# First-layer norms as fused VectorE operations, all masks added by GpSimd, and three of four transposed probability tiles copied by ScalarE

## The chip, the core and the metric

The kernel runs on one core of one Trainium2 chip. Its time is the device time of one execution in microseconds (us); the time before is the median of three runs. A core has TensorE (the matrix engine, PE in the profile, its weight loads PEld), VectorE (DVE), ScalarE (ACT), GpSimd (POOL) and SyncE (SP), which here only issues transfers. The engines run their own instruction queues in order and wait for each other by semaphores.

## The reference

Eight sequences of 512 tokens and width 512 go through four layers. Layer 0 is an adapter with a norm, layer 1 attention and a feed-forward part, layer 2 a feed-forward part with per-sequence weights, layer 3 a stencil. The change touches the two norms ahead of attention and the softmax of attention:

```python
# layer 0
hidden = gelu(x @ down_W.T + down_b)                     # 512 x 128
hidden = hidden @ Wsel + bsel + domain_emb               # expert chosen per sequence
x = hidden @ up_W.T + up_b + x
x = (x - mean(x)) * rsqrt(var(x) + 1e-5) * ln_gamma + ln_beta         # norm 0
# layer 1
x = (x - mean(x)) / sqrt(var(x) + 1e-5) * (1 + scale) + shift         # norm 1
q, k, v = x @ Wq + bq, x @ Wk + bk, x @ Wv + bv          # 16 heads of 32
scores = q @ k.T / sqrt(32) + attention_bias             # per head 512 x 512
scores = where(src_mask, -inf, scores)
ctx = softmax(scores) @ v
x = x + ctx @ Wo + bo
...
```

## The kernel before

The program is two passes. `attention_pass` does layer 0 and attention, sequence by sequence, in a loop of eight iterations; `ffn_pass` does the rest and isn't touched. The first pass runs from about 67 us to 1101 us of the profiled span; ahead of it a prologue prepares weights and does layer 0 and both norms of the first sequence.

**An iteration.** TensorE projects q, k and v, then goes through 20 slots (`SLOTS_ALL`). Slots 0 to 15 each score one query tile of 128 rows for four heads: slot u belongs to head group u // 4 and query tile u % 4. In slot u TensorE makes four score tiles (`scores(u)`, banks 0 to 3 of PSUM), VectorE reads each, adds the bias and takes the minimum of the negated row (line 1000, output `tiles` and `nmax`), and ScalarE exponentiates (line 792). One slot later TensorE transposes the four 128x512 probability tiles (`turn`, line 651; the last of the four yet a slot later), an engine copies each transposed bank into `pT`, and TensorE multiplies by v (`values`, line 642). Beside this, slots carry work listed in `BESIDE`: the projections of the next head groups (slots 2, 3, 6, 7, 10, 11), and layer 0 of the *next* sequence (xT, down, expert, up in slots 0 to 5). VectorE takes the norm's statistics of the next sequence in slots 5 and 6 (norm 0) and 10 and 11 (norm 1). After slot 19 come the output products and the transposes of the normed next sequence.

**The bias.** SyncE loads the attention bias in halves of a slot (two heads, 128x1024 float32, 512 KB), 32 halves per iteration, into a ring of six buffers (`stage`, named `bias` in the code). Half n+6 is issued as soon as VectorE has scored half n.

**The mask.** Half of it goes by GpSimd: for the first half of each slot (heads 0 and 1) GpSimd adds the mask to the bias in place (line 508). For heads 2 and 3 TensorE first writes the mask into the bank by an identity product (line 625) and the scores accumulate on it.

**The norms of the next sequence.** After the statistics, GpSimd computes 1/sqrt(var) by ten small dependent operations and four more (`rstd_of_norm`), ScalarE scales each 128x512 tile (line 724), and GpSimd multiplies by the gain and adds the shift (lines 488 and 489). In the prologue VectorE does the same by `rstd_first` and `norm_first` (lines 917 to 926), two operations per tile.

**The copies into `pT`.** Of the four tiles of a slot VectorE copies 0 and 1 (line 1015) and ScalarE 2 and 3 (line 778).

**What sets the order.** Each engine's program is written out in slot order. Scores of slot u+1 go to the same four banks, so TensorE claims each after VectorE scored that tile of slot u. The bank ring of three for everything else is fixed by `attention_slots`.

Of the kernel before, what the change touches and what calls it, by code (L numbers as in the profile page):

```python
# [26 lines left out]
ALU = mybir.AluOpType  # L27
ACT = mybir.ActivationFunctionType
# [6 lines left out]
LINKS_A = 18  # L35
# [56 lines left out]
def pv_parts(u):  # L92
# [11 lines left out]
ACT_L0 = {8: (("scale0", 0), ("scale0", 1)), 9: (("scale0", 2), ("scale0", 3)),  # L104
          13: (("scale1", 0),), 14: (("scale1", 1),), 16: (("scale1", 2), ("scale1", 3))}
DVE_L0 = {5: (("stats0", 0), ("stats0", 1)), 6: (("stats0", 2), ("stats0", 3)),
          10: (("stats1", 0), ("stats1", 1)), 11: (("stats1", 2), ("stats1", 3))}
POOL_L0 = {2: (("up_bias",),), 9: (("rstd", 0),), 10: (("gain0", 0), ("gain0", 1)), 11: (("gain0", 2), ("gain0", 3)),
           14: (("rstd", 1),)}
# [35 lines left out]
def attention_pass(nc, a, ada_rows, x2_dram, stage, stage_in):  # L145
# [7 lines left out]
    with ExitStack() as ctx:  # L153
# [74 lines left out]
        shift = sb("shift", [P, T], F32)  # L228
# [32 lines left out]
        pool_chain = sem("pool_chain")  # L261
        pool_carrier = sem("pool_wait_carrier")
# [10 lines left out]
        rstd_ready = sem("rstd_ready")  # L273
        scaled0 = sem("scaled0")
        ln0_ready = sem("ln0_ready")
        scaled1 = sem("scaled1")
# [3 lines left out]
        pT_ready = [sem("pT_first_two_ready"), sem("pT_last_two_ready")]  # L280
# [26 lines left out]
        def read_by(key):  # L307
# [5 lines left out]
                    "T": (pT_ready[k // 2], H * T // 2, k % 2), "R": (rinv_T_ready, G, k),  # L313
                    "ctx": (ctx_ready, G, k), "wo": (x2_ready, T, k)}[name]

        def claim(pe, it, key):
# [5 lines left out]
            if last[0] == "T":  # L322
                k += last[1] * T // 2
# [124 lines left out]
        def _(pool):  # L448
# [7 lines left out]
            count = [0]  # L456

            def pool_link(base, ins):
                count[0] += 1
                ins.then_inc(pool_chain, 1)  # L460
                pool.wait_ge(pool_chain, base + count[0])

            def rstd_of_norm(base, q, which):

                def link(ins):
                    pool_link(base, ins)
                    pool.sem_inc(pool_carrier, 1)
# [15 lines left out]
            def gain(it, base, which, t):  # L483

                q = before_it(it)
                times, plus = ((ln_g[:, :], ln_b[:, :]), (ada[:, 0, :], ada[:, 1, :]))[which]
                pool.wait_ge((scaled0, scaled1)[which], q * T + t + 1)
                pool_link(base, pool.tensor_tensor(xin[:, t, :], xin[:, t, :], times, ALU.mult))
                pool.tensor_tensor(xin[:, t, :], xin[:, t, :], plus, ALU.add).then_inc((ln0_ready, x1_ready)[which], 1)

            up_bias(None)
            before_loop = count[0]
            POOL_LINKS = 2 * 15 + 2 * T
            pool.wait_ge(rows_out, 16)
            with pool.Fori(0, B) as it:
                base = before_loop + it * POOL_LINKS
                count[0] = 0

# [6 lines left out]
                for u in range(NQ):  # L505
                    n = 2 * u
# [3 lines left out]
                    for part in POOL_L0.get(u, ()):  # L510
                        if part[0] == "up_bias":
                            up_bias(it)
                        if part[0] == "rstd":
                            rstd_of_norm(base, it + 1, part[1])
# [1336 lines left out]
```

## Time and profile before

| | |
|---|---|
| median of three runs | 2616.97 us (2615.83 to 2617.12) |
| profiled execution | 2614.7 us, its span 2612.9 us |
| busy share of the span | PE 96%, DVE 76%, ACT 44%, POOL 40% |
| granted TensorE clock, mean | 0.989 of full speed |
| chain that ended last | PE 39%, DVE 9%, issue 6%, ACT 1%, POOL 1% |
| one iteration of the attention loop | 129.3 us (the mask conversion, line 958, starts at 67.0 us in the first and at 972.1 us in the last: 905.1 / 7) |

The busy share is an average over both passes. What the loop does has to be read in a stretch of the loop: which engine is never idle there, and how long each engine needs for a slot. A timeline row is: start in us, duration in us, engine, line, operation, output and inputs, count, and in brackets the idle time before it and what ended it. Two instructions of one engine may overlap by the pipeline, so the cost of one in a row of equal ones is the distance of the starts and not its duration.

### The profile page before, as it was taken

Reading aid. Unit: us, or ns where it says so; the run is one execution under the profiler, and the core shown is the slowest. Engines: PE = TensorE matmul, PEld = TensorE weight load, DVE = VectorE, ACT = ScalarE, POOL = GpSimd, SP = SyncE. Lnnn points to the kernel's source line nnn. Section 1 sums busy time; section 2 is a strip of 40 time slices with the busy share of each in tenths; the row PEclk is TensorE's granted clock in tenths of the full one; section 3 lists DMA queues with packets and bytes.
Section 4 is the critical chain, followed back from the end, with each engine's and each line's share of the span. In section 5 each row is a group of like instructions: output and inputs, shape, how many; then the busy total and the mean of one; then the engine's idle time right before and its main releaser. Section 6 shows DMA issues by size and latency. Waiting matters only on the chain.

```text
span 2612.9 us, 47096 instructions
## 1 busy us (share of the span) xinstructions
PE 2497.7 (96%) x14495; PEld 1237.5 (47%) x14583; DVE 1980.6 (76%) x3863; ACT 1147.6 (44%) x2189; POOL 1038.3 (40%) x887
## 2 busy tenths in 40 slices
PE   6999999999999999869999999999999999999996
PEld 4455555555555555434444444444444444444443
DVE  7877777777777777777878688678687786886787
ACT  3666666667666767633322223223222222232331
POOL 1464646464646464524234133143242340431430
PEclk8999999999999999989999999999999999999998
DMA  6444444454545444452322232142222222322340
GB/s 208 144 154 157 156 151 160 146 162 147 167 145 166 146 160 147 141 179 93 113 82 86 90 107 96 54 137 89 90 93 101 98 77 82 130 89 77 102 159 23
DMA packets 155507, 320.56 MB, mean 123 GB/s; under 512 B 17474, under 2 KB 23234, under 8 KB 155218
## 3 DMA queue, kind: packets, MB, share of 16 engines
q1 hardware_dynamic: 145426, 299.13, 34.6%
q10 hardware_dynamic: 9792, 17.83, 1.9%
q8 instruction: 151, 2.47, 0.4%
q14 instruction: 138, 1.13, 0.1%
HBM read 298.85 MB, written 17.86 MB: 121 GB/s over the span
## 4 chain that ended last, share of the span: by engine, by line
PE 39%; DVE 9%; issue 6%; ACT 1%; POOL 1%; DMA 1%; DVEq 0%; ACTq 0%; POOLq 0%
PE ffn_bank L1371 12%; PE ffn_bank L1373 12%; PE ffn_bank L1372 12%; PE ffn_bank L1357 2%; DVE g2T_hi L1686 1%; DVE f L1569 1%; POOL stage L1298 1%; ACT g L1512 1%; DVE stats L1554 1%; PE ffn_bank L1437 1%; PE ffn_bank L1378 1%; DVE w_lo L1656 1%; DVE stage L1597 1%; DVE f L1572 0%; DMA stage<-in_W 0%
## 5 line engine op out<-in xcount | busy, mean ns | idle before, releaser
L1000 DVE CUSTOM_DVE_ANT_0 tiles<-bank,stage 128x512 f32<-128x512 f32 x512 | 323.9, 686 | 79.4 <-PE bank L628 74.8
L792 ACT ACTIVATE tiles<-tiles,nmax 128x512 f32<-128x512 f32 x512 | 363.5, 714 | 44.5 <-DVE nmax L1000 44.4
L508 POOL TENSOR_TENSOR stage<-stage,mask_add 128x1024 f32<-128x1024 f32 x128 | 272.6, 2141 | 203.1 <-DMA stage<-in_bias 183.9
L651 PE MATMUL bank<-ident,tiles 128*128 128x128 f32 x2048 | 300.2, 280 | 16.6 <-ACT pT L778 4.4
L1686 DVE CAST g2T_hi<-g 128x512 f16<-128x512 f32 x256 | 164.8, 644 | 188.7 <-ACT g L1512 181.1
L651 PEld LDWEIGHTS bank<-ident,tiles 128*128 128x128 f32 x2048 | 222.6, 140 | 176.4 <-issue 83.2
L1298 POOL TENSOR_TENSOR stage<-grid,f 128x512 f32<-128x512 f32 x96 | 150.5, 1594 | 284.4 <-DMA grid<-in_grids 175.1
L1687 DVE TENSOR_TENSOR g2T_lo<-g,g2T_hi 128x512 f16<-128x512 f32 x256 | 245.6, 959 | 8.8
L1512 ACT ACTIVATE g<-ffn_bank,bi 128x512 f32<-128x512 f32 x128 | 88.1, 688 | 360.1 <-PE ffn_bank L1373 349.7
L1371 PE MATMUL ffn_bank<-w_hi,g2T_hi 128*128 128x512 f16 x512 | 195.3, 382 | 28.3 <-DVE g2T_lo L1687 28.0
L778 ACT ACTIVATE pT<-bank 128x512 f32<-128x512 f32 x256 | 151.1, 590 | 150.1 <-PE bank L651 150.1
L1312 POOL TENSOR_TENSOR x<-x2n,b 128x512 f32<-128x512 f32 x32 | 39.5, 1269 | 442.3 <-DVE f L1714 442.3
L1305 POOL TENSOR_TENSOR stage<-grid,f 128x512 f32<-128x512 f32 x64 | 106.4, 1681 | 267.0 <-DVE stage L1623 139.6
L1371 PE MATMUL ffn_bank<-x3T_hi,wl_hi 128*128 128x512 f16 x512 | 194.3, 379 | 5.6 <-DVE stage L1631 5.6
L1371 PE MATMUL ffn_bank<-x3T_hi,w_hi 128*128 128x512 f16 x512 | 194.3, 379 | 3.4 <-DVE x3T_lo L1653 3.3
L1372 PE MATMUL ffn_bank<-w_lo,g2T_hi 128*128 128x512 f16 x512 | 195.1, 381 | 0.0
L1373 PE MATMUL ffn_bank<-w_hi,g2T_lo 128*128 128x512 f16 x512 | 195.1, 381 | 0.0
L1372 PE MATMUL ffn_bank<-x3T_lo,w_hi 128*128 128x512 f16 x512 | 194.2, 379 | 0.0
L1371 PE MATMUL ffn_bank<-wl_hi,g2T_hi 128*128 128x512 f16 x512 | 194.0, 379 | 0.0
L1372 PE MATMUL ffn_bank<-wl_lo,g2T_hi 128*128 128x512 f16 x512 | 194.0, 379 | 0.0
L1373 PE MATMUL ffn_bank<-wl_hi,g2T_lo 128*128 128x512 f16 x512 | 194.0, 379 | 0.0
L1373 PE MATMUL ffn_bank<-x3T_hi,w_lo 128*128 128x512 f16 x512 | 194.0, 379 | 0.0
(289 smaller groups left out, 5195.1 us busy)
## 6 DMA issues: line engine op xcount, KB each, us to landing
stage<-in_bias SPq DMA_DIRECT2D x256, 512.0 KB, 4.1
stage<-in_W_l SPq DMA_DIRECT2D x128, 512.0 KB, 3.3
grid<-in_grids SPq DMA_DIRECT2D x160, 256.0 KB, 3.3
xin<-in_x SPq DMA_DIRECT2D x36, 256.0 KB, 4.1
out<-stage ACTq DMA_DIRECT2D x36, 256.0 KB, 2.0
x_rows<-tiles ACTq DMA_DIRECT2D x32, 256.0 KB, 3.0
stage<-in_W SPq DMA_DIRECT2D x16, 512.0 KB, 4.9
x2n<-x_rows SPq DMA_DIRECT2D x8, 1024.0 KB, 7.0
```

Of the source, the lines that this page charges most:

```text
L508: pool.tensor_tensor(bias[:, n % NB, :, :], bias[:, n % NB, :, :], mask_add[:, u % T, :].unsqueeze(1).to_broadcast([P, 2, S]), ALU.add).th ...
L651: mm = pe.transpose(bank[:, t * P:(t + 1) * P], tiles[:, 4 * (u % NR) + i, t * P:(t + 1) * P], ident[:, :])
L778: act.activation(pT[:, (u // 2) % 2, i, :, (u % 2) * P:(u % 2 + 1) * P], bank[:, :].rearrange("p (t q) -> p t q", t=T), ACT.Copy).then_inc ...
L792: act.activation(tile, tile, ACT.Exp, scale=-1.0, bias=nmax[:, u % 2, i:i + 1], accum_out=rsum[:, j, h:h + 1]).then_inc(prob_ready, 1)
L1000: dve.tensor_tensor_reduce(tiles[:, 4 * (u % NR) + i, :], bank[:, :], bias[:, half % NB, i % 2, :], -1.0, 3.0e38, ALU.add, ALU.min, nmax[: ...
L1298: pool.tensor_tensor(prod[:, i, :], grid[:, i, :], f[:, t, :], ALU.mult).then_inc(alpha_prod, 1)
L1371: pe.matmul(out, w[0], x[0], start=first, stop=False)
L1372: pe.matmul(out, w[0], x[1], start=False, stop=False)
L1373: return pe.matmul(out, w[1], x[0], start=False, stop=last)
L1512: act.activation(g32[:, n % 2, :], bank[:, :], func, scale=1.0 / WS, bias=vec[:, n % NF:n % NF + 1]).then_inc(gelu_ready, 1)
L1686: link(dve.tensor_copy(gT[0][:, n % 4, :], g32[:, n % 2, :]))
L1687: dve.tensor_tensor(gT[1][:, n % 4, :], g32[:, n % 2, :], gT[0][:, n % 4, :], ALU.subtract)\
```

## The change

It does five things. (1) The two norms of the next sequence leave GpSimd and ScalarE: VectorE computes 1/sqrt(var) with eleven small operations (`norm_root`) in slots 7 and 12, and does each tile with two fused operations (`norm_tile`) in slots 8 and 9 (norm 0, two tiles a slot) and 13 to 16 (norm 1, one tile a slot). (2) GpSimd adds the mask to both halves of each slot's bias. (3) TensorE's two identity products per slot go. (4) VectorE copies only transposed tile 0, ScalarE tiles 1, 2 and 3. (5) GpSimd's addition of the up-bias moves from slot 2 to behind the masks of slot 4.

```diff
-ACT_L0 = {8: (("scale0", 0), ("scale0", 1)), ...
-DVE_L0 = {5: ..., 6: ..., 10: ..., 11: ...}
-POOL_L0 = {2: (("up_bias",),), 9: (("rstd", 0),), 10: (("gain0", 0), ("gain0", 1)), 11: (("gain0", 2), ("gain0", 3)),
-           14: (("rstd", 1),)}
+DVE_L0 = {5: (("stats0", 0), ("stats0", 1)), 6: (("stats0", 2), ("stats0", 3)), 7: (("rstd", 0),),
+          8: (("norm0", 0), ("norm0", 1)), 9: (("norm0", 2), ("norm0", 3)),
+          10: (("stats1", 0), ("stats1", 1)), 11: (("stats1", 2), ("stats1", 3)), 12: (("rstd", 1), ("ada", 0)),
+          13: (("norm1", 0),), 14: (("norm1", 1),), 15: (("norm1", 2),), 16: (("norm1", 3),)}
...
                 for u in range(NQ):
-                    n = 2 * u
...
+                    for n in (2 * u, 2 * u + 1):
+                        pool.wait_ge(bias_in[n % NB], (it * USES[n % NB] + n // NB + 1) * 16)
+                        pool.tensor_tensor(bias[:, n % NB, :, :], bias[:, n % NB, :, :],
+                                           mask_add[:, u % T, :].unsqueeze(1).to_broadcast([P, 2, S]), ALU.add).then_inc(masked, 1)
+                    if u == 4:
+                        up_bias(it)
...
                     for i in range(4):
-                        bank = claim(pe, it, ("S", u, i))
-                        if i >= 2:
-                            pe.matmul(bank[:, :], ident_bf[:, :], mask_add[:, j, :], start=True, stop=False)
...
+                        claim(pe, it, ("S", u, i))
                         pe.matmul(psum[i][:, :], q32[rows, g, j * P:(j + 1) * P], k32[rows, g, :],
-                                  start=i < 2, stop=True).then_inc(full[i], 1)
+                                  start=True, stop=True).then_inc(full[i], 1)
...
                     if 0 < u <= NQ:
+                        evacuate(u - 1, 1)
                         evacuate(u - 1, 2)
...
+            def norm_root(link, it, which):
+                dve.wait_ge(stats_ready, before_it(it) * 2 * T + which * T + T)
                 dve.sem_inc(carrier, 1)
                 link(dve.tensor_scalar(var[:, :], mv[:, :, 1], 1e-5, None, ALU.add))
                 rsqrt_steps(dve, link, var[:, :], rstd[:, :], newt[:, :], rstd[:, :].bitcast(I32), var[:, :].bitcast(I32))
+            def norm_tile(link, which, t):
                 times, plus = ((ln_g[:, :], ln_b[:, :]), (ada[:, 0, :], ada[:, 1, :]))[which]
                 link(dve.scalar_tensor_tensor(out=xin[:, t, :], in0=xin[:, t, :], scalar=mv[:, t, 0:1], in1=times,
                                               op0=ALU.subtract, op1=ALU.mult))
                 dve.scalar_tensor_tensor(out=xin[:, t, :], in0=xin[:, t, :], scalar=rstd[:, t:t + 1], in1=plus,
                                          op0=ALU.mult, op1=ALU.add).then_inc((ln0_ready, x1_ready)[which], 1)
...
-                            if i == 0:
-                                dve.wait_ge(masked, it * NQ + u + 1)
-                            if i == 2:
-                                dve.wait_ge(bias_in[half % NB], (it * USES[half % NB] + half // NB + 1) * 16)
+                            if i in (0, 2):
+                                dve.wait_ge(masked, it * 2 * NQ + half + 1)
```

VectorE's program in slot 8, before: the last score pair, the reciprocal of the softmax sum, its spread, two copies into `pT`, and the low half of the context (line 978), then slot 9 begins.

```order
L1006 RECIPROCAL rinv<-rsum 128x16
L819 REGISTER_ALU
L1007 COPY rinv_x<-rinv 128x512
L331 REGISTER_ALU
L1015 COPY pT<-bank 128x4x128 x2
L978 REGISTER_ALU
L978 SCALAR_TENSOR_TENSOR xT_lo<-ctx,bv,xT_hi 128x512
L331 REGISTER_ALU
```

The same place in the changed kernel, from the spread (now line 943) on:

```order
L943 COPY rinv_x<-rinv 128x512
L324 REGISTER_ALU
L950 COPY pT<-bank 128x4x128
L915 REGISTER_ALU
L916 SCALAR_TENSOR_TENSOR xT_lo<-ctx,bv,xT_hi 128x512
L862 SCALAR_TENSOR_TENSOR xin<-xin,mv,ln_g 128x512
L759 REGISTER_ALU
L864 SCALAR_TENSOR_TENSOR xin<-xin,rstd,ln_b 128x512
L862 SCALAR_TENSOR_TENSOR xin<-xin,mv,ln_g 128x512
L759 REGISTER_ALU
L864 SCALAR_TENSOR_TENSOR xin<-xin,rstd,ln_b 128x512
```

One copy of 128x512 has gone, and four operations of 128x512 that read two tiles each have come, all ahead of the scores of slot 9.

GpSimd's program from slot 9 to slot 11, before (`stage` is the bias, `var`, `rstd` and `newt` the small operations of the root, of which only the first are shown):

```order
L508 TENSOR_TENSOR stage<-stage,mask_add 128x1024
L468 ISA
L470 TENSOR_SCALAR var<-mv 128x4
L461 ISA
L74 TENSOR_SCALAR rstd<-var 128x4
L461 REGISTER_ALU
L76 TENSOR_TENSOR newt<-rstd 128x4
```

And in the changed kernel from slot 4 on, where nothing but masks is left behind the up-bias:

```order
L454 TENSOR_TENSOR xin<-xin,up_b 128x512 x4
L468 TENSOR_TENSOR stage<-stage,mask_add 128x1024 x2
L467 ISA
L468 TENSOR_TENSOR stage<-stage,mask_add 128x1024 x2
L467 ISA
L468 TENSOR_TENSOR stage<-stage,mask_add 128x1024 x4
```

Every slot's pair of masks stands behind one another there, where before one mask per slot stood between the norm's operations.

## Rows read from the trace of the kernel before

**Rows 1.** The page, part 1: busy us, share of the span, instructions.
```profile
PE 2497.7 (96%) x14495; PEld 1237.5 (47%) x14583; DVE 1980.6 (76%) x3863; ACT 1147.6 (44%) x2189; POOL 1038.3 (40%) x887
```
**Rows 2.** Stretches of one iteration each (the fourth; the sum over eight); columns as named.
```profile
core 0: us, PE busy (x) PEld busy (x) DVE busy (x) ACT busy (x) POOL busy (x), PEclk, DMA share, GB/s
454.90:584.20 129.30, 126.69 (x930) 68.51 (x940) 97.06 (x222) 87.43 (x197) 70.97 (x73) 1.00 0.48 154
...
sum 1034.40, PE 1006.10 PEld 544.24 DVE 780.76 ACT 697.01 POOL 563.23; mean PE 125.76 PEld 68.03 DVE 97.60 ACT 87.13 POOL 70.40
```
**Rows 3.** Groups by line, 0 to 1300 us: busy us, mean ns | idle before.
```profile
L508 POOL TENSOR_TENSOR stage<-stage,mask_add 128x1024 f32<-128x1024 f32 x128 | 272.6, 2141 | 203.1 <-DMA stage<-in_bias 183.9 <-DVE mask_add L958 19.1
...
L1015 DVE COPY pT<-bank 128x512 f32<-128x512 f32 x256 | 164.4, 683 | 6.8 <-PE bank L651 6.8
L778 ACT ACTIVATE pT<-bank 128x512 f32<-128x512 f32 x256 | 151.1, 590 | 150.1 <-PE bank L651 150.1
...
L724 ACT ACTIVATE xin<-xin,shift,rstd 128x512 f32<-128x512 f32 x64 | 49.3, 808 | 0.0
```
**Rows 4.** PE timeline: a slot's identity and score products; score products of slots 7, 15.
```profile
428.04 0.59 PE L625 MATMUL bank<-mask_add,ident_bf 128*128 128x512 bf16 x2
428.56 1.14 PE L628 MATMUL bank<-k,q 32*128 32x512 f32 x8
...
512.12 1.14 PE L628 MATMUL bank<-k,q 32*128 32x512 f32 x8
...
557.99 1.14 PE L628 MATMUL bank<-k,q 32*128 32x512 f32 x8
```
**Rows 5.** DVE timeline of slots 6 to 9.
```profile
507.93 0.69 DVE L1000 CUSTOM_DVE_ANT_0 tiles<-bank,stage 128x512 f32<-128x512 f32 x1
...
512.01 0.68 DVE L891 BATCH_NORM_STATS2 stats<-xin 128x6 f32<-128x512 f32 x1
...
514.11 0.69 DVE L1000 CUSTOM_DVE_ANT_0 tiles<-bank,stage 128x512 f32<-128x512 f32 x1 [0.17 <-issue]
...
523.12 0.25 DVE L1006 RECIPROCAL rinv<-rsum 128x16 f32<-128x16 f32 x1
523.40 0.43 DVE L1007 COPY rinv_x<-rinv 128x512 f32<-128x512 f32 x1
...
524.94 0.74 DVE L978 SCALAR_TENSOR_TENSOR xT_lo<-ctx,bv,xT_hi 128x512 f16<-128x512 f32 x1
525.60 0.68 DVE L1000 CUSTOM_DVE_ANT_0 tiles<-bank,stage 128x512 f32<-128x512 f32 x1
```
**Rows 6.** POOL timeline: a mask after its transfer; a small operation in slot 12.
```profile
512.40 2.13 POOL L508 TENSOR_TENSOR stage<-stage,mask_add 128x1024 f32<-128x1024 f32 x1 [5.32 <-DMA stage<-in_bias]
...
547.94 0.48 POOL L76 TENSOR_TENSOR newt<-rstd 128x4 f32<-128x4 f32 x1 [0.18 <-POOL rstd L80]
```
**Rows 7.** DVE timeline of the prologue: norm 1 of the first sequence.
```profile
45.95 0.17 DVE L917 TENSOR_SCALAR var<-mv 128x4 f32<-128x4 f32 x1
...
48.26 0.75 DVE L923 SCALAR_TENSOR_TENSOR xin<-xin,mv,ada 128x512 f32<-128x512 f32 x1 [0.16 <-DVE rstd L83]
49.16 0.75 DVE L926 SCALAR_TENSOR_TENSOR xin<-xin,rstd,ada 128x512 f32<-128x512 f32 x1 [0.16 <-DVE xin L923]
...
50.72 1.53 DVE L926 SCALAR_TENSOR_TENSOR xin<-xin,rstd,ada 128x512 f32<-128x512 f32 x1
```
**Rows 8.** POOL timeline of the prologue at the same time.
```profile
50.06 1.64 POOL L503 TENSOR_TENSOR x<-xin,bo 128x512 f32<-128x512 f32 x1 [32.11 <-DVE xin L926]
```
**Rows 9.** POOL timeline: masks back to back in two places.
```profile
586.08 6.35 POOL L508 TENSOR_TENSOR stage<-stage,mask_add 128x1024 f32<-128x1024 f32 x3 [1.26 <-DVE mask_add L958]
...
606.72 6.46 POOL L508 TENSOR_TENSOR stage<-stage,mask_add 128x1024 f32<-128x1024 f32 x3
```
**Rows 10.** DVE timeline at those two places.
```profile
588.43 2.01 DVE L868 SCALAR_TENSOR_TENSOR exp_eff<-ident,invalid,exp_eff 128x128 f32<-128x128 f32 x1
590.47 2.04 DVE L870 TENSOR_SCALAR wexp_hi<-exp_eff 128x128 f16<-128x128 f32 x1
...
606.84 0.69 DVE L1000 CUSTOM_DVE_ANT_0 tiles<-bank,stage 128x512 f32<-128x512 f32 x1
```

More of the change, by code:

```diff
@@ L33 @@
 U8 = mybir.dt.uint8
-LINKS_A = 18
+LINKS_A = 48
 LINKS_B = 134
@@ L322, in claim @@
             if last[0] == "T":
-                k += last[1] * T // 2
+                k += last[1] * (3 if last[2] else 1)
             pe.wait_ge(signal, base.get(signal, 0) + it * per + (0 if banks.first[key] else k + 1))
@@ L505, in _ @@
                 for u in range(NQ):
-                    n = 2 * u
-                    pool.wait_ge(bias_in[n % NB], (it * USES[n % NB] + n // NB + 1) * 16)
-                    pool.tensor_tensor(bias[:, n % NB, :, :], bias[:, n % NB, :, :],
-                                       mask_add[:, u % T, :].unsqueeze(1).to_broadcast([P, 2, S]), ALU.add).then_inc(masked, 1)
[L510 to L514, printed above, removed]
-                        if part[0] == "gain0":
-                            gain(it, base, 0, part[1])
-                pool.wait_ge(ada_in, it * 16 + 32)
-                for t in range(T):
-                    gain(it, base, 1, t)
+                    for n in (2 * u, 2 * u + 1):
[4 more added lines that the diff above has]
+                        up_bias(it)
         @block.tensor
@@ L636, in values @@
                         pe.wait_ge(v32_ready, 1 + it * T + T)
-                        for half in range(2):
-                            pe.wait_ge(pT_ready[half], 1 + it * (HT // 2) + 4 * v + 4)
+                        pe.wait_ge(pT_ready[0], 1 + it * NQ + 2 * v + 2)
+                        pe.wait_ge(pT_ready[1], 1 + it * 3 * NQ + 3 * (2 * v + 2))
                     cols = slice((v % 2) * 2 * P, (v % 2) * 2 * P + 2 * P)
@@ L719, in l0_part @@
                         .then_inc(hid_ready, 1)
-                if key[0] in ("scale0", "scale1"):
-                    which, t = int(key[0] == "scale1"), key[1]
-                    act.wait_ge(rstd_ready, q * 2 + which + 1)
-                    act.activation(xin[:, t, :], xin[:, t, :], ACT.Identity, scale=rstd[:, t:t + 1],
-                                   bias=shift[:, t:t + 1]).then_inc(scaled1 if which else scaled0, 1)
             def weight_hi(i):
```

80 lines of the change are left out of this document (20 added, 60 removed).

## The prediction

> **What bounds the kernel now.** I read the shares of the page first [rows 1]: TensorE 96%, the others far below. That says nothing of a slot, so next came the stretches of one iteration [rows 2]: in 129.30 us TensorE is busy 126.69, VectorE 97.06, ScalarE 87.43, GpSimd 70.97, at granted clock 1.00, and all eight are alike (mean 125.76, 97.60, 87.13, 70.40). So the loop is bound by TensorE, with 2.6 us of idle. The timelines give the slot. A slot with nothing beside it takes TensorE 4.55 us; in it the two identity products of the mask start at 428.04 and the score products behind them at 428.56, so they cost 0.52 us [rows 4]. The stretch that the change loads most, from the score products of slot 7 (512.12) to those of slot 15 (557.99), takes 45.87 us [rows 4].
>
> In what follows s(u) is the time at which VectorE begins to score slot u, S(u) that at which TensorE begins the score products.
>
> **What goes.** 0.52 us of TensorE in each of 16 slots, 8.3 us per iteration, 66.6 us in eight. If TensorE stayed the bound, the time would be 2614.7 - 66.6 = 2548.
>
> **What ScalarE gets.** 16 more copies of 0.59 us and 8 scalings of 0.81 us less [rows 3]: 9.4 - 6.5 = +2.9 us on 87.4 us, in 129. It stays below TensorE's 118 to 121 and I cost it at nothing; in a slot without anything beside it ScalarE needs four exponentials and three copies, a little over TensorE's new 4.03 us, which matters only in the slots where VectorE, below, is later anyway.
>
> **What VectorE gets, if nothing hinders it.** Scoring costs 0.61 us a tile (starts), 2.45 a slot, and a copy 0.60. It loses 16 copies (-9.6). It gets two roots: the first small operation of the prologue's starts at 45.95 and the first tile operation at 48.26, 2.3 us each [rows 7]. It gets eight tiles of two operations: 48.26 to 49.16, and 0.67 more, 1.56 us a tile, 12.5 together. Sum +7.5 us on 97: still less than TensorE's 118, but not slot by slot. The rest of a slot must be done before the next can be scored, and TensorE can be ahead only by one set of score banks. Per slot, in order: slot 7: 2.45 scoring + 0.67 k + 0.6 copy + 2.3 root = 6.0; slot 8: 2.45 + 0.62 (reciprocal and spread, 523.12 to 523.74) + 0.6 + 0.66 (line 978, 524.94 to 525.60) + 3.1 = 7.4; slot 9: 6.2; slots 10 and 11: 5.75, with statistics of 2.1 for two tiles (512.01 to 514.11); slot 12: 2.45 + 0.62 + 0.6 + 0.66 + 2.3 = 6.6; slot 13: 4.6; slot 14: 5.2 [rows 5]. TensorE needs 4.03 in slots 8, 12 and 14 and about 4.5 in 9 and 13.
>
> **The walk without hindrance.** Clock at S(7) = 0. The statistics of slot 6 wait for the context, which is 9.1 us behind S(6), and S(7) is now 6.62 behind S(6), so s(7) = 2.5 (before: 514.11 - 512.12 = 2.0). Then s(8) = 8.5, s(9) = 15.9, s(10) = 22.1, s(11) = 27.9, s(12) = 33.6, s(13) = 40.2, s(14) = 44.8, and S(15) follows the scores of slot 14, at 47.2: 1.4 us *more* than the 45.87 of before. Only slots 0 to 6 would gain, 7 x 0.52 = 3.6. That makes -2.2 us an iteration, 2597 us. It is a rival below.
>
> **The hindrance.** Two rows show VectorE's norm operation at two prices. At 49.16 line 926 took 0.75 us; at 50.72 the same operation on the next tile took 1.53 [rows 7], and GpSimd ran a tile addition from 50.06 to 51.70 [rows 8]. At 588.43 and 590.47 operations of only 128x128 took 2.01 and 2.04 us, each ending 0.1 us behind the end of one of three masks that GpSimd ran back to back from 586.08 in 2.12 us each [rows 9, 10]. The scoring operation, which reads a bank and one tile, is not touched: 0.69 us at 606.84 under a mask that began at 606.72. So an operation of VectorE that reads two SBUF tiles (or copies within SBUF) waits until GpSimd's running instruction ends, then runs, then the next mask goes ahead of the next such operation: they take turns. That is a price of up to 2.14 us for each mask that meets such work. The same lock holds the other way: GpSimd's small operation at 547.94 took 0.48 us while VectorE spread the reciprocal [rows 6]; I take from this that small operations ask for it as well.
>
> The Trainium skill, "SBUF — State Buffer", section "Who interferes with whom", says that a VectorE instruction with two SBUF inputs contends with a GpSimd instruction that reads SBUF, and that the later one fully blocks until the first has finished. The trace agrees (1.53 against 0.75 us). By this rule alone the norms placed on VectorE and the masks doubled on GpSimd obstruct each other; without it the sum would be the 2597 of the walk above.
>
> **Where the masks fall.** A half released by scoring at 508.54 (the second tile began at 507.93 [rows 5]) is masked from 512.40 [rows 6], 3.86 us later; the release is 1.2 us behind s(u). So GpSimd starts at s(u) + 5.0 and now does two masks, until s(u) + 9.3 or later. VectorE's two-input work begins 3 us behind s(u). Slots of 6 to 8 us put masks and norms on each other.
>
> The walk with turns. Slot 7: the root runs from 6.2, the masks start at 7.5; one small operation gets in between the two, the rest behind the second: s(8) = 12.7, +4.2. Slot 8: norm tiles from 17.0, masks from 17.7; the second operation waits 2.1, the third again: s(9) = 24.3, +4.2. Slot 9: only the last operation meets a mask, +2.0: s(10) = 32.5. Slots 10 and 11 have statistics (one input), nothing added: s(11) = 38.3, s(12) = 44.1. Slot 12: the spread waits 0.8, then the root meets both masks, +4.3: s(13) = 55.7. The masks end with the half released in slot 12, so slots 13 and 14 are free: s(14) = 60.3, S(15) = 60.3 + 2.45 = 62.7. Against 45.87 that is +16.9 us.
>
> At the loop's start GpSimd now masks six halves in a row from 586.08, where it did three. The last two of the five small expert operations, at 592.54 and later, ran free; now each can wait for a mask, s(0) comes 1.9 to 3.8 us later, and TensorE, which has v and two transposes beside, gives back about 2 of it. In slots 2 and 3 a cast can wait as well, under 9 and 7 us of TensorE: nothing. The up-bias in slot 4 is ready some 2 us ahead of its use (the masks of slot 4 start 5 us behind s(1)); if it were late, up to 2 us.
>
> **The sum.** Per iteration +16.9 (slots 7 to 14) - 3.6 (slots 0 to 6) + 2 (start) = +15.3 us; the tail behind slot 15 has the same TensorE work. Eight iterations: +122, so 2614.7 + 122 = 2737 for the profiled execution, which stands 2.3 us below the median of the runs (its span is 1.8 shorter still). I take 2735. GpSimd itself is no bound: 32 x 2.14 + 8 x 1.27 = 79 us in 145.
>
> Bounds of what the trace doesn't show. Whether the root's tiny operations (128x4) wait: nothing if they don't, then slots 7 and 12 lose 8.5 us of the 16.9; 2.1 per mask met if they do; I take the second by the 128x128 rows. Whether the turn always goes to the waiting mask: if VectorE could run on, slot 8 would cost 2.1 instead of 4.2, -17 us in eight; the prologue's operations don't tell. How long the later masks take to arrive: 3.86 us is one transfer that had its twin 1.2 us behind, as now; a us later moves the masks further into the norms of slots 8 and 9, at most +2 per slot, +32 in eight.
>
> **Rivals.**
> 1. The tiny operations don't wait. Per iteration 15.3 - 8.5 = +6.8: 2614.7 + 54, about 2670. For it: no row shows a 128x4 operation of VectorE held. Against: the 0.48 us at 547.94.
> 2. No collisions of weight: the masks fall beside scoring and copies and GpSimd ends ahead of the norms. Then the walk without hindrance, 2597, faster. It would take less than 2.2 us of waiting per iteration, one single mask met; the walk has seven. Against it also stands s(u) + 5.0 in slots that VectorE itself needs 6 to 7 us for.
> 3. Only TensorE counts and VectorE's slots are smoothed by the score banks: 2548. Against: slot 8 needs 7.4 us against 4.03 with nothing in between.
> 4. More than forecast: VectorE's stalls leave TensorE idle for up to 7 us at a stretch, and its granted clock, 1.00 all through the loop [rows 2], falls. Slots 10 and 11 with their projections (6.62 each at full clock) would be the first to feel it; at half clock they and the products behind slot 19 cost some 10 us an iteration more: 2815. Nothing in the loop of before shows a fall.
> 5. The halves cancel: rival 1 with fewer turns lost than walked, within 0.2% of before.
>
> **Chances.** Forecast (2700 to 2790) 0.55; rival 1 (2640 to 2700) 0.25; rival 4 0.05; rivals 2 and 3 0.07; between, 2620 to 2640, 0.04; within 0.2% 0.04 (about what three runs of this kernel can tell from no change). Range 2650 to 2790. Faster 0.07, same 0.04, slower 0.89.
>
> **What would show it.** Scores, copies and statistics on VectorE keep their 0.69, 0.68 and 0.67 us, but the tile operations of the norms have a mean well over 0.75, with a mode near 2.1 to 2.9; the root's small operations in slots 7 and 12 show single ones of 2 us; the identity products are gone; the iteration is about 144.5 us with TensorE busy near 118 and idle in slots 8, 9, 12 and 13 ahead of the score products, released by VectorE; slots 0 to 6 are no longer than before. I am wrong if the norm operations stay at 0.75, if the iteration comes below 131, or if the loss lies in slots 0 to 6 or in waits for the masks themselves.

## The result and the profile after

The changed kernel takes 2779.6 us (median of four runs, 2778.7 to 2784.0) against 2616.4 (2615.0 to 2617.1): ratio 1.0629, 95% interval 1.0613 to 1.0644. That is 163 us more, where 118 were forecast; 2779.6 lies inside the range. The span of the profiled execution is 2776.9 us. From here on times are of profiled executions where they are of slots and iterations, and medians where they are of kernels. Times of single slots are of the fourth iteration unless another is named.

The page's first part, to be read beside [rows 1]:

```profile
PE 2579.1 (93%) x14327; PEld 1283.7 (46%) x14327; DVE 2150.2 (77%) x4039; ACT 1172.4 (42%) x2253; POOL 1101.3 (40%) x631
```

TensorE has 168 products fewer in these records (256 weight loads fewer, which is what the change takes away; some products of the kernel before are missing from its records) and is busy 81 us *longer*, a sign to look at its clock. The fourth stretch of one mean iteration and the sum over eight such stretches, to be read beside [rows 2] (us, then busy time of each engine, granted clock, DMA share, GB/s):

```profile
515.20:665.00 149.80, 136.37 (x908) 73.66 (x907) 119.51 (x244) 90.46 (x205) 79.42 (x40) 0.93 0.41 133
...
sum 1198.40, PE 1086.08 PEld 590.90 DVE 954.73 ACT 721.55 POOL 629.14; mean PE 135.76 PEld 73.86 DVE 119.34 ACT 90.19 POOL 78.64
```

The iteration went from 129.3 to 149.8 us; 8 x 20.5 = 164 us, the whole loss. What follows the eighth iteration takes 1512.7 us, before 1511.5. VectorE is busy 119 us instead of 97, where its own additional work was 7.5. The clock is 0.93 instead of 1.00.

The groups by line over the whole span (busy us, mean ns | idle before) say where VectorE's time went:

```profile
L468 POOL TENSOR_TENSOR stage<-stage,mask_add 128x1024 f32<-128x1024 f32 x256 | 553.6, 2173 | 305.4 <-DMA stage<-in_bias 283.3 <-DVE mask_add L896 20.0
...
L936 DVE CUSTOM_DVE_ANT_0 tiles<-bank,stage 128x512 f32<-128x512 f32 x512 | 323.8, 686 | 50.2 <-PE bank L575 32.2 <-POOL stage L468 6.9 <-DVE rstd L83 6.6
...
L864 DVE SCALAR_TENSOR_TENSOR xin<-xin,rstd,ln_b 128x512 f32<-128x512 f32 x36 | 56.0, 1556 | 1.3
...
L83 DVE SCALAR_TENSOR_TENSOR rstd<-newt,rstd 128x4 f32<-128x4 f32 x108 | 34.5, 320 | 3.7
...
L864 DVE SCALAR_TENSOR_TENSOR xin<-xin,rstd,ada 128x512 f32<-128x512 f32 x36 | 29.7, 826 | 1.3
```

Scoring keeps 0.686 us, and in the whole run it waited only 6.9 us for masks that were not done: late masks are not the loss. Norm 0's second tile operation has a mean of 1556 ns, norm 1's 826: the same instruction, but norm 0 stands in slots 8 and 9 beside masks and norm 1 in slots 13 to 16, where the masks are done.

Slots 7 and 8 on VectorE (start, duration), to be read beside [rows 5]:

```profile
586.06 0.16 DVE L82 SCALAR_TENSOR_TENSOR newt<-newt,var 128x4 f32<-128x4 f32 x1
586.25 2.01 DVE L83 SCALAR_TENSOR_TENSOR rstd<-newt,rstd 128x4 f32<-128x4 f32 x1
...
588.69 2.10 DVE L83 SCALAR_TENSOR_TENSOR rstd<-newt,rstd 128x4 f32<-128x4 f32 x1
591.16 0.69 DVE L936 CUSTOM_DVE_ANT_0 tiles<-bank,stage 128x512 f32<-128x512 f32 x1 [0.37 <-DVE rstd L83]
...
595.49 0.75 DVE L862 SCALAR_TENSOR_TENSOR xin<-xin,mv,ln_g 128x512 f32<-128x512 f32 x1
596.27 2.59 DVE L864 SCALAR_TENSOR_TENSOR xin<-xin,rstd,ln_b 128x512 f32<-128x512 f32 x1
598.79 2.61 DVE L862 SCALAR_TENSOR_TENSOR xin<-xin,mv,ln_g 128x512 f32<-128x512 f32 x1
601.44 0.75 DVE L864 SCALAR_TENSOR_TENSOR xin<-xin,rstd,ln_b 128x512 f32<-128x512 f32 x1
602.11 0.68 DVE L936 CUSTOM_DVE_ANT_0 tiles<-bank,stage 128x512 f32<-128x512 f32 x1
```

GpSimd in the same stretch:

```profile
586.10 2.14 POOL L468 TENSOR_TENSOR stage<-stage,mask_add 128x1024 f32<-128x1024 f32 x1 [2.99 <-DMA stage<-in_bias]
588.65 2.12 POOL L468 TENSOR_TENSOR stage<-stage,mask_add 128x1024 f32<-128x1024 f32 x1 [0.41 <-DMA stage<-in_bias]
596.18 2.14 POOL L468 TENSOR_TENSOR stage<-stage,mask_add 128x1024 f32<-128x1024 f32 x1 [5.41 <-DMA stage<-in_bias]
598.47 2.38 POOL L468 TENSOR_TENSOR stage<-stage,mask_add 128x1024 f32<-128x1024 f32 x1 [0.15 <-DMA stage<-in_bias]
```

Lay the two beside each other. An operation over four columns, 0.16 us a moment ago, starts 0.15 us behind a mask and ends with it (588.26 and 588.24). The next two run in the gap; the second mask starts at 588.65, 0.04 us ahead of the operation at 588.69, which ends with it. In slot 8 each of two masks holds one tile operation. Scoring, at 591.16 and 602.11, stands behind them.

Slot 12 has the same with norm 1's root (VectorE, then GpSimd):

```profile
627.82 2.11 DVE L857 TENSOR_SCALAR var<-mv 128x4 f32<-128x4 f32 x1
...
630.16 2.08 DVE L76 TENSOR_TENSOR newt<-rstd 128x4 f32<-128x4 f32 x1
```
```profile
627.73 2.17 POOL L468 TENSOR_TENSOR stage<-stage,mask_add 128x1024 f32<-128x1024 f32 x1 [1.37 <-DMA stage<-in_bias]
630.10 2.13 POOL L468 TENSOR_TENSOR stage<-stage,mask_add 128x1024 f32<-128x1024 f32 x1 [0.20 <-DMA stage<-in_bias]
```

And the start of an iteration (VectorE, then GpSimd), beside [rows 9, 10]:

```profile
524.71 2.00 DVE L808 SCALAR_TENSOR_TENSOR exp_eff<-ident,invalid,exp_eff 128x128 f32<-128x128 f32 x1
...
530.97 1.97 DVE L813 SCALAR_TENSOR_TENSOR exp_bias<-exp_vec,valid 128x1 f32<-128x1 f32 x1
```
```profile
522.36 12.65 POOL L468 TENSOR_TENSOR stage<-stage,mask_add 128x1024 f32<-128x1024 f32 x6 [1.26 <-DVE mask_add L896]
```

Four operations wait where it was two, one of them over a single column.

TensorE's score products of slots 8, 10 and 14, beside [rows 4]:

```profile
585.13 1.14 PE L575 MATMUL bank<-k,q 32*128 32x512 f32 x8
...
602.85 3.90 PE L575 MATMUL bank<-k,q 32*128 32x512 f32 x8 [2.88 <-DVE nmax L936]
...
635.03 3.90 PE L575 MATMUL bank<-k,q 32*128 32x512 f32 x8 [4.15 <-DVE nmax L936]
```

The rows name VectorE as the one that TensorE waited for. But eight products that took 1.14 us now take 3.90. The stretches around them tell why (columns as above):

```profile
597.00:602.85 5.85, 2.98 (x29) 1.99 (x28) 5.82 (x6) 0.62 (x2) 3.70 (x2) 0.93 0.08 32
602.85:608.00 5.15, 5.15 (x13) 2.37 (x14) 5.08 (x11) 4.04 (x11) 1.07 (x1) 0.67 0.50 167
608.00:614.60 6.60, 6.60 (x40) 3.18 (x38) 5.42 (x11) 4.42 (x11) 3.79 (x2) 0.74 0.36 117
630.00:635.00 5.00, 0.88 (x12) 0.42 (x4) 4.24 (x13) 0.00 (x0) 2.13 (x1) 1.00 0.00 0
635.00:639.00 4.00, 3.97 (x9) 1.92 (x10) 3.96 (x10) 3.89 (x10) 0.00 (x0) 0.54 0.01 4
639.00:643.40 4.40, 4.40 (x32) 3.21 (x32) 3.30 (x10) 3.39 (x10) 0.00 (x0) 0.64 0.00 0
```

TensorE, idle for 4.12 of the 5.00 us from 630, gets 0.54 of full speed in the four after it, close to its lower level (1.2 of 2.4 GHz), and 0.64 in the next 4.4. From 643.4 it is at 1.00 again.

### The profile page after: what moved, and what is told of

The parts are those of the page before. It is cut to its first block and busy times, and to the rows that moved or that the text cites. A ratio compares the mean times of both kernels' runs of the same rounds, so it can differ in the third digit from the quotient of the medians.

```text
span 2776.9 us, 46456 instructions
## 1 busy us (share of the span) xinstructions
PE 2579.1 (93%) x14327; PEld 1283.7 (46%) x14327; DVE 2150.2 (77%) x4039; ACT 1172.4 (42%) x2253; POOL 1101.3 (40%) x631
## 5 line engine op out<-in xcount | busy, mean ns | idle before, releaser
L468 POOL TENSOR_TENSOR stage<-stage,mask_add 128x1024 f32<-128x1024 f32 x256 | 553.6, 2173 | 305.4 <-DMA stage<-in_bias 283.3
L598 PE MATMUL bank<-ident,tiles 128*128 128x128 f32 x2048 | 319.8, 295 | 26.0 <-DVE pT L950 13.6
L598 PEld LDWEIGHTS bank<-ident,tiles 128*128 128x128 f32 x2048 | 241.2, 149 | 200.5 <-issue 113.8
L575 PE MATMUL bank<-k,q 32*128 32x512 f32 x1024 | 225.6, 706 | 80.7 <-DVE nmax L936 80.7
L719 ACT ACTIVATE pT<-bank 128x512 f32<-128x512 f32 x384 | 213.8, 588 | 106.0 <-PE bank L598 105.3
```

The source lines that it names most:

```text
L468: pool.tensor_tensor(bias[:, n % NB, :, :], bias[:, n % NB, :, :], mask_add[:, u % T, :].unsqueeze(1).to_broadcast([P, 2, S]), ALU.add).th ...
L575: pe.matmul(psum[i][:, :], q32[rows, g, j * P:(j + 1) * P], k32[rows, g, :], start=True, stop=True).then_inc(full[i], 1)
L598: mm = pe.transpose(bank[:, t * P:(t + 1) * P], tiles[:, 4 * (u % NR) + i, t * P:(t + 1) * P], ident[:, :])
L719: act.activation(pT[:, (u // 2) % 2, i, :, (u % 2) * P:(u % 2 + 1) * P], bank[:, :].rearrange("p (t q) -> p t q", t=T), ACT.Copy).then_inc ...
```

## The experiments

Of the kernel before, the same jobs have medians of 2613.0 to 2614.2 us. "Iteration" is the mean length between the mask conversions of the first and the eighth.

### The changed kernel without masks

```
-   pool.wait_ge(bias_in...); pool.tensor_tensor(bias, bias, mask_add, ALU.add).then_inc(masked, 1)   # both halves
-   if i in (0, 2): dve.wait_ge(masked, it * 2 * NQ + half + 1)
+   if i in (0, 2): dve.wait_ge(bias_in[half % NB], (it * USES[half % NB] + half // NB + 1) * 16)
```


> The changed kernel without GpSimd's mask additions (the masks are left out altogether; VectorE waits for the bias transfer instead). VectorE's instructions are all as in the changed kernel. Theory (turns at the SBUF port): the walk without hindrance, 2597, less about 1 us an iteration at the loop's start, so 2590 (2570 to 2610), norm operations of 0.75 us throughout, none near 2. Rival A (VectorE has simply too much work per slot): nothing VectorE does is gone, so within 30 us of 2780. Rival B (TensorE's clock is the cause, the stalls only its trigger): follows the theory here, since without stalls the clock stays; told apart by the rows of the clock.

2627.8 us, ratio 1.0056 (1.0039 to 1.0073), iteration 130.64. Taking away GpSimd's masks alone gives back 152 of 163 us: the loss needs the masks, and since scoring hardly waits for them, it is their meeting with VectorE. No norm or root operation is held in this trace. VectorE's additional work isn't free either: the identity products are worth 0.43 us in each of 16 slots (a slot with nothing beside it went from 4.55 to 4.12 us), 6.9 us an iteration, and this kernel doesn't gain them but takes 1.3 us more.

The expectation of 2570 to 2610 was missed by 18 us. The stretch from S(7) to S(15) takes 48.7 us, where the walk without hindrance has 47.2 and the kernel before 45.87. Up to s(10) the walk holds (22.1 behind S(7) forecast, 21.8 measured); then s(11) is 1.1 us late, and in these two stretches behind S(10) TensorE is never idle and its clock is down:

```profile
525.80:530.90 5.10, 5.10 (x16) 2.34 (x17) 5.03 (x11) 4.38 (x11) 0.00 (x0) 0.81 0.56 191
530.90:536.00 5.10, 5.10 (x38) 2.66 (x37) 3.76 (x11) 3.98 (x10) 0.00 (x0) 0.85 0.49 148
```

Slot 10, whose projections make it 6.7 us without the identity products, took 10.2. So rival 2's walk of VectorE was right to 1.5 us and its gain was not: against its -2.2 us an iteration this kernel has +1.35. By means over the iterations slots 7 to 14 gave +2.7 instead of +1.4, slots 0 to 6 -2.9 instead of -3.6, and what follows slot 15 +1.6 instead of nothing.

### Half of the masks

```
-   for n in (2 * u, 2 * u + 1):  mask by GpSimd
+   for n in (2 * u,):            mask by GpSimd
+   if i >= 2: pe.matmul(bank, ident_bf, mask_add[:, j, :], start=True, stop=False)
```


> The changed kernel with the masks as before: GpSimd adds them to the first half of each slot, TensorE writes the others by the identity product. Norms on VectorE and three copies on ScalarE stay. Theory: one mask per slot from 5.0 us behind the start of scoring, so one turn of 2.1 us lost in slots 7, 8 and 12 and perhaps 9, and slots of TensorE as before: from the scores of slot 7 to those of slot 15 about 54.5 us against 45.9 before, so +69 us, 2685 (2660 to 2710). Rival A: VectorE's work is the same as in the changed kernel and TensorE's is more: 2780 or above.

2729.5 us, ratio 1.0442 (1.0425 to 1.046), iteration 141.87, S(7) to S(15) 57.5 us. Half of the masks cost more than half of the loss: a miss of 45 us. The meetings themselves came as expected: four operations in the stretch from S(7) to S(15) are held, 7.3 us together. 24 of the 45 us are in this stretch (3 us an iteration), where the granted clock was 0.88 and 0.76 in slots 9 and 10; 15 us are in the second pass, whose code is the same: what follows the eighth iteration took 1526.6 us in this profile, and 1506 to 1514 in all others but one.

### The norms back on GpSimd and ScalarE, all masks kept

The kernel before with the changed kernel's mask loop and waits, no identity products, and copies one and three.

> Norms as before on GpSimd and ScalarE; all masks on GpSimd, no identity products, three copies on ScalarE as in the change. Theory: VectorE meets no mask with two-input work in slots 7 to 12, but GpSimd now has 32 masks of 2.14, 16 norm operations of 1.28, two roots of 6.1 and ten us of additions, 111 us of some 121, and in slots 9 to 15 52 us against 34 of TensorE with 6 us of lead: it comes about 12 us late, against 8.3 us that TensorE saves: +4 us an iteration, 2650 (2600 to 2700), waits for the masks ahead of scoring. Rival A (the norms on VectorE cost nothing by the port): no difference to the changed kernel beyond their 15 us of VectorE.

2701.3 us, ratio 1.033 (1.0313 to 1.0347), iteration 140.76. This is 1 us above the expected range. All masks on GpSimd, with the three copies, cost 11.5 us an iteration even with the norms in their old place. Part of it is a queue and not a meeting: root 1, sixteen small operations in GpSimd's rows, stands ahead of two masks.

```profile
585.85 6.97 POOL L508 TENSOR_TENSOR stage<-stage,mask_add 128x1024 f32<-128x1024 f32 x3
592.91 0.23 POOL L470 TENSOR_SCALAR var<-mv 128x4 f32<-128x4 f32 x1
...
598.85 4.21 POOL L508 TENSOR_TENSOR stage<-stage,mask_add 128x1024 f32<-128x1024 f32 x2
```

The mask that scoring of slot 15 needs starts 5.9 us late; S(15) comes 11.0 us behind S(14), where it was 4.55. Moving the root to VectorE takes this wait away, but there it meets masks.

### The changed kernel without the loop's roots

Leaves out 1/sqrt(var) in the loop; one operation writes ones.

```
-   link(dve.tensor_scalar(var[:, :], mv[:, :, 1], 1e-5, None, ALU.add));  rsqrt_steps(...)
+   link(dve.tensor_scalar(rstd[:, :], mv[:, :, 1], 0.0, 1.0, ALU.mult, ALU.add))
```


> The changed kernel with the eleven small operations of each root in the loop replaced by one that writes ones (the norms of sequences 2 to 8 are not divided by their deviation; nothing else is left out). Theory with small operations taking turns too: slot 7 loses 4.2 + 2.1 us, slot 12 as much, some of it hidden under TensorE's 6.6 us in slot 7: -10 us an iteration, 2700 (2680 to 2720). Rival (small operations never wait, only the tile operations do): -2 to -4 us an iteration, 2750 to 2765.

2718.7 us, ratio 1.0399 (1.0375 to 1.0423): 61 us less than the changed kernel, for 20 operations an iteration that need 0.2 us each when free: 8 x 20 x 0.2 = 32 us if nothing else counted. S(7) to S(15) is 55.6 us instead of 65.0; 55 of the 61 us are in the loop by the length of the iterations. This and the held rows of slots 7 and 12 show that the tiny operations do wait for masks; rival 1 is out.

### The norms in the gaps between masks

The changed kernel, with the root right behind the last scoring operation of slot 7, norm 0's tiles in the same place in slots 8 to 11, and the second statistics, root and tiles in slots 13 to 17.

```
+   if i == 4:
+       for part in DVE_EARLY.get(u, ()):  norm_root(...) or norm_tile(...)
```


> The changed kernel with the same instructions and other places for the norms: root 0 right behind the scoring of slot 7, one tile of norm 0 right behind the scoring of slots 8 to 11, statistics of norm 1 in slots 13 and 14, root 1 in slot 15 and its tiles in 16 and 17, where no mask is left and VectorE is idle. Theory (the price is made of masks met and of slots overfilled, both a matter of place): about one turn of 2.1 us each in slots 8 and 9, nothing else, from the scores of slot 7 to those of slot 15 some 50 us (the changed kernel 65): 2650 (2625 to 2680). Rival A (VectorE's load as such): VectorE does exactly the same work, no gain over 2780 beyond 20 us.

2698.9 us, ratio 1.032 (1.03 to 1.0339), iteration 140.10. The stretch came out as forecast, 49.1 us against 50, with the root free of masks:

```profile
554.09 0.16 DVE L83 SCALAR_TENSOR_TENSOR rstd<-newt,rstd 128x4 f32<-128x4 f32 x1
```

The same instructions with the same masks on GpSimd, only at another moment, give back 16 us in this stretch. About 5 of them are root 1 and two tiles of norm 1, now behind S(15). The rest fits the meetings: over their free durations, VectorE's operations took 13.8 us too long in this stretch of the changed kernel (eight of them) and 3.5 us here (two, 564.31 and 574.45, 2.5 us each instead of 0.75). The whole did not follow, and 2698.9 lies above the expected range: S(0) to S(7) took 52.8 us (50.7 in the changed kernel), and from S(15) to the next iteration's score products it was 2.9 us more in the mean (37.2 for 34.3), where VectorE's norm tiles now stand behind slot 15.

### The small expert operations later

The kernel of the last section, with the five expert operations at the end of slot 1 instead of ahead of slot 0.

> The run with other places for the norms (2698.9), and the five small expert operations of VectorE moved from ahead of the scores of slot 0 to the end of slot 1, where no mask runs. Theory (at the loop's start four of the five wait a whole mask each, TensorE stalls and its clock falls): the stretch from the scores of slot 0 to those of slot 2 takes 17.9 us there and 12.9 in the kernel before; it falls back to 13 or 14, so 4 to 5 us an iteration, 2660 to 2667. Rival A (load): the same five operations, no change.

2706.7 us (2698.0 to 2717.4), ratio 1.0367 (1.034 to 1.0393), where 2660 to 2667 was expected. S(0) to S(2) fell from 17.9 to 12.5 us as forecast, and S(2) to S(4) rose from 16.7 to 23.7. In slot 1 GpSimd has masks and then the four additions of the up-bias, and all five operations are held: two by masks, three for 1.1 to 1.25 us by the up-bias (VectorE, then GpSimd):

```profile
508.03 2.01 DVE L808 SCALAR_TENSOR_TENSOR exp_eff<-ident,invalid,exp_eff 128x128 f32<-128x128 f32 x1
```
```profile
505.68 4.22 POOL L468 TENSOR_TENSOR stage<-stage,mask_add 128x1024 f32<-128x1024 f32 x2 [0.36 <-DMA stage<-in_bias]
509.85 5.05 POOL L454 TENSOR_TENSOR xin<-xin,up_b 128x512 f32<-128x512 f32 x4
```

### Only the copies

The kernel before, with VectorE copying tile 0 and ScalarE 1, 2 and 3.

```
-   for i in (0, 1):   VectorE copies;   evacuate(u - 1, 2)
+   for i in (0,):     VectorE copies;   evacuate(u - 1, 1);  evacuate(u - 1, 2)
```


> The kernel before with one part of the change alone: ScalarE copies three of the four transposed tiles, VectorE one. Theory (the copies are off the path, TensorE bounds the loop): within 5 us of before. Rival C (the copies are part of the loss: ScalarE copies tile 1 only behind the four exponentials, so TensorE waits for the bank): 0.5 us or more a slot, 60 us slower.

2635.8 us, ratio 1.0079 (1.0064 to 1.0095): 22 us slower, where at most 5 were expected. 12 us are in the loop (iteration 130.81, +1.5): slot 9 takes 6.14 us for 5.72 and slot 10 7.32 for 7.14, and most of the rest is lost behind S(15). In all TensorE waits 2.7 us an iteration for ScalarE's copies, where it was 0.5. One of these waits, in slot 9, is for a copy that stands behind two norm scalings (528.10, 1.51 us together) on ScalarE:

```profile
530.15 0.66 PE L651 MATMUL bank<-ident,tiles 128*128 128x128 f32 x4 [0.93 <-ACT pT L778]
```

The other 12, by the profiled execution, are in the second pass (1523.5 us against 1511.5), which the edit doesn't touch; no run tells why.

### The changed kernel with the copies two and two

> The changed kernel with the copies two and two again (VectorE copies tiles 0 and 1). Alone, three copies on ScalarE cost the kernel before 22 us. Theory (in the changed kernel VectorE bounds slots 8, 9 and 12 to 14): VectorE's extra copy costs 0.6 us in each of these slots and in the stretch before slot 7 nothing, against 2.8 us an iteration that it gives back: about the same, 2770 to 2800. Rival C (the copies on ScalarE are a main part of the loss): 2700 or below.

2814.6 us, ratio 1.0761 (1.0744 to 1.0777), 35 us slower than the changed kernel and above the expected range. The iteration is 5.3 us longer, with S(10) to S(11) of 13.6 to 14.1 us for 11.2 to 11.9. So giving ScalarE a third copy costs 22 us by itself (12 of them in the loop) and saves 35 beside the norms. A likely reason is that where VectorE sets the end of a slot its copy of 0.6 us goes straight to the path; no run takes the copies of single slots apart.

### Both masks by GpSimd in some slots

Four mixtures: the kernel before, with both halves masked by GpSimd (and no identity products) in a set of slots only.

```
+ DOUBLE = (6, 7, 8)
-   n = 2 * u
+   for n in ((2 * u, 2 * u + 1) if u in DOUBLE else (2 * u,)):
-   if i >= 2:                         # identity product
+   if i >= 2 and u not in DOUBLE:
```

Slots 3 to 8:

> The kernel before with one thing of the change, and only in slots 3 to 8: there GpSimd adds both masks and TensorE's identity products go; norms and copies as before. Theory: GpSimd has room there (its mask there waits for the transfer), VectorE's work in these slots reads banks or one tile but for one cast pair and two spreads, and TensorE bounds: 6 x 0.52 x 8 = 25 us less, 2590 (2586 to 2598). If masks doubled were themselves the loss (rival D, GpSimd late or transfers late): same or slower than before.

2616.0 us, ratio 1.0008 (0.9999 to 1.0017): no change, and not the forecast. Slots 4, 5 and 7 each give their 0.43 us, but slot 3 takes 9.9 to 11.3 us for 8.3. In the kernel before, one mask holds the cast of slot 2 (2.10 us at 482.16) and the subtraction behind it runs free in 0.69. Here masks stand back to back behind the up-bias and hold both (GpSimd, VectorE, TensorE):

```profile
479.84 13.23 POOL L509 TENSOR_TENSOR stage<-stage,mask_add 128x1024 f32<-128x1024 f32 x6
```
```profile
484.47 1.98 DVE L882 CAST ctx<-rinv_T 128x512 f16<-128x512 f32 x1 [2.57 <-ACT rinv_T L713]
486.48 2.50 DVE L883 TENSOR_TENSOR ctx<-rinv_T,ctx 128x512 f16<-128x512 f32 x1
```
```profile
489.64 0.66 PE L652 MATMUL bank<-ident,tiles 128*128 128x128 f32 x4 [2.20 <-DVE pT L1020]
```

Slots 3 to 8 and 13 to 15, with root 1 behind the masks:

> As the one before, and both masks also in slots 13 to 15, with GpSimd's root of norm 1 moved behind the masks of slot 15. Theory: 9 x 0.52 x 8 = 37 us less if GpSimd keeps up, 2577; GpSimd has in slots 9 to 15 ten masks of 2.14, a root of 6.1 and 10.3 us of gains, 38 us, against 32 to 34 of TensorE and 6 of lead, so it may be late by a few us in slot 15: 2577 to 2610. Rival D: slower than before.

2672.3 us, ratio 1.0223 (1.0209 to 1.0237). Slots 13 and 14 took 5.4 to 7.4 and 7.6 to 10.2 us for 5.1 and 4.55: a forecast that missed its sign.

Slots 5 to 8:

> As the one before, with slot 5 too. Its second mask is done in slot 3 to 4 behind the three masks that before has back to back as well. Theory: 4 x 0.43 x 8 = 14 us less, 2600 (2596 to 2606), or 2 to 3 us above that if the slot-3 cast meets it.

2618.3 us, ratio 1.0016 (1.0007 to 1.0025), where at most 2606 was expected, or 2 to 3 us above that. The second mask of slot 5 meets the subtraction. This run holds its own comparison: in six iterations both the cast and the subtraction were held and slot 3 took 10.1 to 11.9 us; in the other two only one of them was held, as before, and it took 8.3 to 8.4.

Slots 6 to 8:

> The kernel before with both masks on GpSimd in slots 6 to 8 only (no identity products there). In the run with slots 3 to 8 the gain of 0.43 us a slot appeared from slot 4 on, and six masks back to back held VectorE's cast and subtraction of slot 2 for 3.4 us more. Theory (the loss there was the masks of slots 3 and 4 meeting two-input work in slot 2): the masks of slots 6 to 8 are done in slots 4 to 7, where VectorE has none but a spread, so 3 x 0.43 x 8 = 10 us less, 2604 (2600 to 2608). Rival D (doubled masks are a loss wherever they stand): within 3 us of before.

2605.6 us (median of six, 2604.4 to 2607.9), ratio 0.9966 (0.9954 to 0.9979): 8.7 us faster than the kernel before, inside the range forecast for this run, and the best of the study. TensorE's slots 5 and 6 on this kernel:

```profile
494.56 0.59 PE L626 MATMUL bank<-mask_add,ident_bf 128*128 128x512 bf16 x2
495.09 1.14 PE L629 MATMUL bank<-k,q 32*128 32x512 f32 x8
500.94 1.14 PE L629 MATMUL bank<-k,q 32*128 32x512 f32 x8
```

Slot 5 takes 5.85 us instead of 6.28 and the iteration 128.27 instead of 129.30. In these runs the masks were worth moving only where VectorE has scores, copies out of PSUM and statistics beside them.

## Why the prediction was right, and where it was short

**Slower, and by this mechanism: right.** The walk of slots 7 to 14 stands against the trace, in us behind S(7) = 578.42:

| | s(7) | s(8) | s(9) | s(10) | s(11) | s(12) | s(13) | s(14) | S(15) |
|---|---|---|---|---|---|---|---|---|---|
| forecast | 2.5 | 12.7 | 24.3 | 32.5 | 38.3 | 44.1 | 55.7 | 60.3 | 62.7 |
| measured | 2.7 | 12.7 | 23.7 | 31.4 | 38.5 | 44.3 | 55.9 | 60.4 | 65.0 |

The prediction counts seven meetings in its walk, and eight are in the trace of slots 7 to 14, one of them 0.7 us long. The agreement isn't the same in every iteration: over the eight, S(15) comes 61.9 to 65.1 us behind S(7), 64.0 in the mean. In the fifth and sixth only one operation of the root in slot 7 is held, s(8) is 10.8 and 10.9 and S(15) 62.0 and 61.9. That the turn goes to the waiting mask (17 us of the bounds) is shown by slot 8, where two operations in a row are held; that tiny operations ask for the lock (8.5 us an iteration) by slots 7 and 12 and by the run without roots. The tile operations' two modes, 0.75 and 2.5 to 2.6 us, were forecast as 0.75 and 2.1 to 2.9.

**The sum was 45 us short.** Forecast +15.3 us an iteration, measured +20.5, which makes 42 us. Most of the rest is a slip: the profiled execution stands 2.3 us *below* the median, so 2737 leads to 2739 and not to the 2735 taken. By terms, in the fourth iteration (means over the eight: slots 7 to 14 +18.1, slots 0 to 6 and the start +2.2, behind slot 15 +0.3):

- *Slots 7 to 14*: +16.9 forecast, +19.15 measured. All of the 2.2 us is in the last step, "S(15) follows the scores of slot 14". VectorE was done in time (its scoring at 638.77 puts S(15) at 641.2), but TensorE was not: its slot at clock 0.54 to 0.64 took 8.4 us and set S(15) to 643.4. In slot 10 the same happened, hidden in the table: TensorE was busy throughout at 0.67 and 0.74, and VectorE waited 1.2 us for it, which made up for 1.1 us by which the walk had been late.
- *Slots 0 to 6 and the start*: -3.6 + 2 = -1.6 forecast, +1.3 measured (50.66 against 49.35 us). Slots 2 to 6 gained 2.0 for the 2.6 counted: the identity products were priced at 0.52 us by the distance of two starts, and a slot gives back 0.43. The term "+2 for the start" is the one that was mis-sized: slots 0 and 1 took 16.2 us where they had 12.9, and where the run without masks has 12.5. That is 3.8 us for the masks there. Four of the small operations were held, as the upper bound of the text allowed, and s(0) came 5.1 us behind S(0); the claim that TensorE "gives back about 2 of it" did not hold: none of it came back, and the granted clock was 0.77 and 0.88 in the two stretches of five us from the score products of slot 1 (533.60) on.
- *ScalarE's copies at nothing*: wrong. Alone they cost 22 us, 12 of them in the loop; beside the norms they save 35. The 9.6 us taken off VectorE's work held up; "ScalarE stays below TensorE" was an argument by totals for a wait within two slots.

**The rivals.** Rival 1 (2670), rival 3 (2548) and rival 5 (no change) are refuted. Rival 2's walk is right to 1.5 us without masks, 48.7 for 47.2, but its time is not: without any meeting the kernel took 2627.8 us and not 2597. Rival 4 had a chance of 0.05 as a case of its own and was in part true at the same time as the forecast: clock and stalls aren't alternatives. Behind each of the three idles of TensorE in slots 7 to 14 (2.60, 2.88 and 4.15 us long, ending at 591.91, 602.85 and 635.03) the granted clock was lower: 0.75, 0.68 and 0.53 in the five us after. A clock term of about 2 us an iteration, what slot 14 lost, belonged in the sum. The row "1.00 all through the loop" told only of a loop without such idles.

**How much is the meeting.** The kernel with the norms in the gaps has every operation of the changed kernel and only another order, and its iteration is 9.7 us shorter. It still has meetings of its own, at the loop's start and in slots 8 and 10. The most is the 19.2 us of the run without masks. Neither is a pure measure: the other order also puts one tile in a slot where there were two, and in both numbers the lower clock behind the stalls is contained.

Open: why the second pass was 12 and 15 us longer in two builds, and how much of the remaining loss at the loop's start is clock and how much waiting.

## What to carry to other kernels

Before moving work to VectorE or GpSimd, list which VectorE operations read two SBUF tiles, or run a copy, cast or `tensor_scalar` within SBUF, and walk both engines by slot: a meeting costs up to the rest of the GpSimd instruction (1.75 to 1.95 us of 2.14 in seven of the eight meetings of slots 7 to 14), whether VectorE's operation has 512 columns or four. Moving such an operation to another moment moves the meeting, so look for a stretch in which VectorE has none of these; three slots of masks moved into such a stretch gave the only gain here, 8.7 us. Where the walk leaves TensorE idle, as in slots 8, 9 and 13 here (2.6 to 4.2 us), charge the slot behind it for a lower clock as well.

## What the hardware showed that I had not expected

Which of VectorE's operations wait isn't told by size or by the count of inputs. A one-input `tensor_scalar` on four columns (2.11 us at 627.82) is held, and a two-input operation on one column (1.97 us at 530.97, where it took 0.22 us before, at 592.87). The statistics, which also read only SBUF, are not held. VectorE, then GpSimd at that time:

```profile
579.97 0.69 DVE L831 BATCH_NORM_STATS2 stats<-xin 128x6 f32<-128x512 f32 x1 [0.20 <-issue]
```
```profile
578.87 4.24 POOL L468 TENSOR_TENSOR stage<-stage,mask_add 128x1024 f32<-128x1024 f32 x2 [1.40 <-DMA stage<-in_bias]
```

The Trainium skill, "SBUF — State Buffer", section "Who interferes with whom", has this distinction: copies, casts and `tensor_scalar` can use the shared port with one input when they run in a two-port mode. I had read it for two inputs only. The trace agrees: the `tensor_scalar` with one input took 2.11 us, and the statistics, which aren't in that list, 0.69. No run shows which mode the small operation ran in.

Masks that stand back to back get ahead of VectorE again and again: 12.65 us of them held four operations that took 0.22 to 0.35 us each in the run without masks. Where GpSimd is idle between two masks, small operations do pass (two between 588.26 and 588.65).

TensorE's granted clock fell after short idles in a kernel that is 93% busy: to 0.54 in the four us after a stretch with 4.12 us idle of 5.00, and to 0.67 after 2.87 of 5.85. In the run without masks it was 0.81 in the first half of slot 10, and the idle just ahead was 0.57 us; an idle of 1.35 us ahead of 563.82 in the same iteration left it at 1.00. So the length of the one idle just ahead doesn't tell.
